# A convolution-attention-expert kernel: two token norms move from GpSimd to ScalarE, the weight products of the opening move behind the first projections, and 35 instead of 41 outward products are plain

## The chip, the cores and the metric

The kernel runs on one core of a Trainium2 chip. The metric is device time in microseconds, median of several runs. The engines are TensorE (PE in the profile; PEld is its weight load), VectorE (DVE), ScalarE (ACT), GpSimd (POOL) and SyncE (SP, which issues most DMAs). Each runs its own instruction stream; they wait for each other by semaphores.

## The reference

Input x is 4 images of 128 channels by 1024 positions, float32. Per image:

1. Group norm over 32 groups of 4 channels, projections q, k, v, full attention of 1024 by 1024 (softmax over 1024 keys), output projection, residual: `x + Wp(softmax(q k / sqrt(C)) v)`.
2. The 1024 positions become tokens `t`. `t = t + attn(ln(t))` with a linear attention of 4 heads: softmax of the keys over the tokens, a context of 32 by 32 per head, output weights and bias b_out.
3. `t = t + moe(ln(t))`: with w = ln(t), 8 experts, router softmax, the best two kept and normed to 1, `out = w + sum_e share_e * (gelu(w W1_e + b1_e) W2_e + b2_e)`. `ln` is `(v - mean) / sqrt(var + 1e-5)` over the 128 channels of a token.

So the first token norm gives `u` (from t1), the second one gives `w_n` (from t2), and `t2 + w_n` is the residual that the experts' sum is added to.

## The kernel before

Tokens of an image are 8 tiles of 128 tokens (TILES = 8, QUAD = 4 of them in a half of 512). Most products are made in two parts, a float32r high part and a low part (value minus high part): `product3` (L1344) issues three matmuls of 512 columns, hi*hi, hi*lo, lo*hi. A "plain" product is one float32 matmul, which the trace records twice.

**Setup and batch 0.** TensorE makes the group means and variances of image 0, then products without use (`keep_busy`, L1373, two records each), then the transpose of Wv, the product `wpv` = Wv Wp and the column `bias_o` (L1385 to L1391), `keep_busy` again, and waits for the first low half of h. Batch b then projects q and k (L1535 to L1544), and for each of 8 score tiles TensorE makes scores (L1409), VectorE the row maximum (L972), ScalarE the exponential (L665), TensorE the transposes (L1418), ScalarE the high copy (L671), VectorE the low part (L977); `attend` (L1423) multiplies with v. Batch 0 also carries the group norm statistics of images 1 to 3: `group_stats`, `channel_means`, `group_deviation`, `group_variance`, `group_affine` on VectorE (L866 to L899), two small products on TensorE, `group_rstd` on GpSimd (L513).

**Pipelining.** Batch b carries the linear attention of image b-1 and the norm, logits and routing of image b-2. GpSimd computes the group-normed input of the next batch (`norm_x`, L527), `add_bias`, and the two token norms: `layer_norm` (L543) makes three small columns (L549 to L553) and then 8 tile instructions (L557); `normed_residual` (L565) adds w_n to t2; `add_bout` (L572) adds the bias. Order within each engine is that of the code.

**Expert stage.** 64 steps, 16 per image (half h, expert e). Step s: TensorE's `hidden` (L1615) into one of two score banks, which needs the gelu of step s-2; then `outward` (L1625) of step s-5 (LAG = 5); ScalarE's `gelu` (L797); VectorE's `weigh` (L1230, gelu times the share of the expert). If the step is not in WHOLE, ScalarE's `high` (L805) and VectorE's `lower` (L1249) make the two parts and `outward` is a product3; if it is in WHOLE, `outward` is plain (L1636). What remains of images 2 and 3 (linear attention, second norm, logits, routing) is put between the steps by the tables TAIL_AT and END_AT: a name and the step behind which each engine does its part of it. POOL_AT orders GpSimd's part the same way, though it only sets an order, since GpSimd takes no part in the steps. Names: PV attend, o output of the linear attention, st the second norm's statistics, OT and OTst the attention output and the first norm's statistics, w0/w1 and u0/u1 the transposes of w_n and u, lg logits, lT logits transposed, rA, rB, rC routing, kT keys, exp both exponentials (another table than gelu's), p transposes of the keys' exponential, g and c the context and the combine weights, z the residual's transposes. Combine weights are stored to DRAM and loaded back as shares, broadcast over the partitions (SyncE, L414).

## Time and profile before

| what | us |
|---|---|
| median of 3 runs (345.7 to 347.02) | 346.47 |
| the profiled execution's own time | 347.13 |
| span of its trace | 345.4 |
| TensorE busy | 310.6 |
| VectorE busy | 248.0 |
| ScalarE busy | 186.4 |
| GpSimd busy | 101.7 |

The span is from the first to the last instruction; the execution's own time has some 1.7 us around it. Times in rows are microseconds from the span's start. A matmul's end is modelled, so TensorE's busy time is not its work at full speed: records of 0.39 us that start every 0.23 us are one after another. The clock column is the granted TensorE clock as a share of 2.4 GHz. Idle time stands in brackets, with what ended it.

### The profile page before, as it was taken

The page shows a single profiled execution, that of the slowest core. Times are in us where ns is not written, and L with a number is a line of the kernel's source. Part 1 is how long each engine was busy: PE and PEld are TensorE (multiplying, and loading weights), DVE is VectorE, ACT ScalarE, POOL GpSimd, SP SyncE. Part 2 cuts the span into 40 slices and gives each one's busy share as a digit, 9 for nine tenths or more (in the row PEclk, how much of TensorE's full clock was granted, in tenths as well). Part 3 has the DMA queues.
Part 4 walks back from the last instruction along what each step waited for, and adds up shares of the span by engine and source line. Part 5 has one row for each costly group of instructions (what it writes and reads, how often), then busy time and mean ns, then how long its engine had stood idle before and what let it go on. Part 6 is the DMA issues. An engine that isn't in the chain of part 4 may idle for free.

```text
span 345.4 us, 5132 instructions
## 1 busy us (share of the span) xinstructions
PE 310.6 (90%) x1573; PEld 240.4 (70%) x1573; DVE 248.0 (72%) x574; ACT 186.4 (54%) x323; POOL 101.7 (29%) x154
## 2 busy tenths in 40 slices
PE   3969998979989889888988998999999997799996
PEld 2858776867878777676877786866557655466784
DVE  4977557497478598978688877597396576846995
ACT  1427546357462568346176658335466334745883
POOL 3806700029400944700446200059420055000000
PEclk9998998998999999999999999999999999989999
DMA  6701000010000020100000108295410691278111
GB/s 176 260 1 62 0 1 2 0 61 3 0 2 1 0 63 9 53 13 0 0 0 0 61 14 261 83 415 198 161 62 0 215 373 47 61 284 325 58 39 61
DMA packets 12756, 29.57 MB, mean 86 GB/s; under 512 B 2192, under 2 KB 5952, under 8 KB 10816
## 3 DMA queue, kind: packets, MB, share of 16 engines
q1 hardware_dynamic: 11872, 29.00, 23.6%
q10 hardware_dynamic: 864, 0.33, 0.4%
q8 instruction: 10, 0.16, 0.2%
q14 instruction: 10, 0.08, 0.1%
HBM read 24.73 MB, written 4.59 MB: 85 GB/s over the span
## 4 chain that ended last, share of the span: by engine, by line
PE 56%; DVE 21%; ACT 8%; issue 7%; POOL 6%; DMA 1%; DVEq 0%; POOLq 0%; ACTq 0%
PE ring L1347 7%; PE ring L1348 6%; PE ring L1349 6%; PE ring L1362 6%; PE scores L1347 5%; PE scores L1349 5%; PE scores L1348 5%; PE ring L1636 5%; DVE row_max L974 5%; DVE pT_lo L980 3%; ACT prob L668 2%; POOL w_n L557 2%; PE ring L1496 2%; DVE lst L1010 2%; ACT pT_hi L674 2%
## 5 line engine op out<-in xcount | busy, mean ns | idle before, releaser
L802 ACT ACTIVATE gel<-scores,b_c 128x512 f32<-128x512 f32 x64 | 43.6, 688 | 44.1 <-PE scores L1349 40.2
L980 DVE TENSOR_TENSOR pT_lo<-ring,pT_hi 128x512 fp32r<-128x512 f32 x64 | 41.2, 683 | 21.0 <-ACT pT_hi L674 20.7
L668 ACT ACTIVATE prob<-scores,row_max 128x1024 f32<-128x1024 f32 x32 | 35.8, 1118 | 25.7 <-DVE row_max L974 25.7
L974 DVE TENSOR_REDUCE row_max<-scores 128x1 f32<-128x1024 f32 x32 | 38.8, 1214 | 11.6 <-PE scores L1349 11.6
L549 POOL TENSOR_SCALAR rstd<-lmv 128x8 f32<-128x8 f32 x8 | 2.2, 270 | 148.5 <-DVE lmv L1016 148.4
L1362 PE MATMUL ring<-ident,prob 128*128 128x128 f32 x256 | 37.1, 287 | 8.0 <-DVE pT_lo L980 2.6
L1362 PEld LDWEIGHTS ring<-ident,prob 128*128 128x128 f32 x256 | 30.5, 147 | 14.1 <-issue 4.1
L674 ACT ACTIVATE pT_hi<-ring 128x512 fp32r<-128x512 f32 x64 | 35.1, 596 | 7.7 <-PE ring L1362 7.6
L1347 PE MATMUL scores<-wT_hi,w_hi 128*128 128x512 f32 x64 | 36.5, 570 | 0.0
L1347 PE MATMUL scores<-k_both,q_hi 128*128 128x512 f32 x64 | 28.2, 441 | 1.0 <-DVE k_both L964 1.0
L1347 PE MATMUL ring<-pT_hi,v_hi 128*128 128x512 f32 x64 | 26.8, 418 | 0.3 <-issue 0.2
L1348 PE MATMUL scores<-k_both,q_hi 128*128 128x512 f32 x64 | 25.9, 404 | 0.0
L1349 PE MATMUL scores<-k_both,q_lo 128*128 128x512 f32 x64 | 25.8, 403 | 0.0
L1349 PE MATMUL scores<-wT_hi,w_lo 128*128 128x512 f32 x64 | 25.5, 398 | 0.0
L1348 PE MATMUL scores<-wT_lo,w_hi 128*128 128x512 f32 x64 | 25.4, 397 | 0.0
L1349 PE MATMUL ring<-pT_hi,v_lo 128*128 128x512 f32 x64 | 25.0, 390 | 0.0
L1348 PE MATMUL ring<-pT_lo,v_hi 128*128 128x512 f32 x64 | 24.9, 390 | 0.0
L678 ACT ACTIVATE o_s<-ring 128x512 f32<-128x512 f32 x8 | 4.8, 598 | 31.6 <-PE ring L1349 31.6
L1347 PEld LDWEIGHTS scores<-wT_hi,w_hi 128*128 128x128 f32 x64 | 12.2, 191 | 7.6 <-issue 5.3
L557 POOL TENSOR_SCALAR w_n<-t,rstd 128x128 f32<-128x128 f32 x32 | 16.8, 539 | 0.9 <-POOL rstd L553 0.9
L1348 PEld LDWEIGHTS scores<-wT_lo,w_hi 128*128 128x128 f32 x64 | 12.3, 192 | 6.4 <-issue 5.5
L1636 PE MATMUL ring<-h_f,w_s 128*128 128x512 f32 x32 | 16.3, 591 | 0.0
(278 smaller groups left out, 707.7 us busy)
## 6 DMA issues: line engine op xcount, KB each, us to landing
pT_hi<-scratch_s SPq DMA_DIRECT2D x8, 1024.0 KB, 5.7
prob<-scratch_s SPq DMA_DIRECT2D x4, 1024.0 KB, 7.1
k_both<-scratch_s SPq DMA_DIRECT2D x3, 1024.0 KB, 6.3
z_in<-scratch_z SPq DMA_DIRECT2D x8, 256.0 KB, 3.0
out_dram<-out_s SPq DMA_DIRECT2D x8, 256.0 KB, 2.2
xb<-in_x_dram SPq DMA_DIRECT2D x3, 512.0 KB, 3.3
scratch_z<-out_s SPq DMA_DIRECT2D x2, 512.0 KB, 2.8
k_both<-scratch_s SPq DMA_DIRECT2D x4, 256.0 KB, 4.5
```

What stands on the lines that cost most here:

```text
L557: last = pool.tensor_scalar(dst[:, j, :], src[:, j, :], neg[:, j:j + 1], std[:, j:j + 1], ALU.add, ALU.mult)
L668: act.activation(prob[:, i % 2, :], scores[:, 2 * (i % 2):2 * (i % 2) + 2, :].rearrange("p a t -> p (a t)"), ACT.Exp, bias=row_max[:, i:i ...
L674: act.activation(tile_group(pT_hi, n, i), as_tiles(ps(place, unit)), ACT.Copy).then_inc(p_hi_made, 1)
L802: act.activation(half(gel, s % 2), scores[:, s % 2, :], ACT.Gelu, bias=b1_c[:, s % E:s % E + 1]).then_inc(e_gelu, 1)
L974: dve.tensor_reduce(row_max[:, i:i + 1], scores[:, 2 * (i % 2):2 * (i % 2) + 2, :].rearrange("p a t -> p (a t)"), AX.X, ALU.max, negate=Tr ...
L980: dve.tensor_tensor(tile_group(pT_lo, n, i), as_tiles(ps(place, unit)), tile_group(pT_hi, n, i).bitcast(FP32), ALU.subtract).then_inc(drai ...
L1010: last = dve.bn_stats(lst[:, j, :], src[:, j, :])
L1347: pe.matmul(dst, lh, rh, start=start, stop=False)
L1348: pe.matmul(dst, lh, rl, start=False, stop=False)
L1349: return pe.matmul(dst, ll, rh, start=False, stop=stop)
L1362: last = pe.transpose(dst[0:t.shape[-1], j * step:j * step + rows], t, ident[0:rows, 0:rows])
L1636: last = pe.matmul(dst, tile(w2_s, e), hs_ring[step % RING], start=False, stop=e == E - 1)
```

## The change

The columns of the two token norms stay on GpSimd in the expert stage (`norm_small`); the tiles are made on ScalarE, as an activation Identity with the column 1/std as scale and -mean/std as bias, in halves of four tiles (`norm_half`, at aw0, aw1, au0, au1). The residual `t2 + w_n` is made on ScalarE too, from t2 with the scale 1/std + 1 and the same bias (`normed_residual`, az), without reading w_n. In batches 1 to 3 GpSimd does the norms as before. In the opening, the three weight products move behind the first projections, ten `keep_busy` products stand in one row, and the group norm of images 1 to 3 moves to later tiles of batch 0. GpSimd's `group_rstd` for these moves behind both expert splits. ScalarE's exponential 1 of batch 0 stands ahead of its v copies. The tables of the expert stage are new, and WHOLE has 35 steps instead of 41. The diff, cut:

```diff
-SETUP_UNITS = ["gn_mean", "gn_var", "wvT", "wpv", "bias_o"]
+SETUP_UNITS = ["gn_mean", "gn_var"]
...
-TAIL_AT = dict(m3=0, PV=1, o=2, st=5, OT=6, OTst=6, w0=12, w1=13, lg=14, u0=15, u1=19, lT=18, rA=19, kT=20, exp=21, rB=21, ks=21, z=19, p=22, rC=23, g=24, c=25)
-END_AT = dict(ctx=25, m2=27, m3=28, o=29, st=29, w0=34, w1=35, lg=36, lT=36, rA=36, exp=37, rB=36, rC=38, z=39, c=39)
+TAIL_AT = dict(m3=0, PV=0, o=2, st=2, OT=5, OTst=5, w0=11, w1=11, lg=13, u0=13, u1=13, lT=15, rA=16, kT=19, exp=19, rB=19, ks=22, z=16, p=20, rC=19, g=22, c=23,
+               aw0=5, aw1=7, au0=9, au1=9, az=8)
+END_AT = dict(ctx=25, m2=27, m3=28, o=29, st=29, w0=34, w1=34, lg=36, lT=38, rA=38, exp=38, rB=38, rC=39, z=41, c=41,
+              aw0=32, aw1=33, az=35)
...
-POOL_AT = dict(n2=4, n1=9, nr=8, ab=18, n2e=30, nre=38)
-
-
-WHOLE = frozenset((2, 3, 4, 5, 6, 7, 8, 9, 10, 11, 12, 13, 14, 15, 16, 17, 18, 19, 20, 21, 22, 23, 24, 25, 26,
-                   27, 28, 29, 30, 31, 32, 33, 34, 37, 38, 39, 40, 42, 43, 44, 45))
+POOL_AT = dict(n2=0, n1=1, ab=2, n2e=3)
+
+
+WHOLE = frozenset((2, 3, 4, 5, 6, 7, 8, 11, 12, 14, 15, 16, 17, 22, 23, 24, 26, 27, 28, 29, 30, 32, 33, 34,
+                   35, 36, 37, 38, 39, 40, 42, 43, 44, 45, 47))
...
+            def norm_small(n, lb):
+
+                eps, std, neg = (rstd[n][:, i, :] for i in range(3))
+                pool.wait_ge(ln_stats[n], lb + 1)
+                pool.tensor_scalar(eps, lmv[n][:, :, 1], 1.0, LN_EPS, ALU.mult, ALU.add
+                                   ).then_inc(ln_small[n], 1)
+                pool.tensor_scalar(neg, lmv[n][:, :, 0], -1.0, 0.0, ALU.mult, ALU.add)
+                pool.wait_ge(ln_small[n], lb * 2 + 1)
+                pool.tensor_tensor(std, eps, minus_half[:, :], ALU.pow).then_inc(ln_small[n], 1)
+                pool.wait_ge(ln_small[n], lb * 2 + 2)
+                after(pool.tensor_tensor(eps, neg, std, ALU.mult))
+                if n == 1:
+                    after(pool.tensor_scalar(neg, std, 1.0, 1.0, ALU.mult, ALU.add))
+                pool.sem_inc(ln_ready[n], 1)
...
-            wait_drained(pool, SETUP, "bias_o")
+            wait_drained(pool, FIRST, "bias_o")
...
-                if name == "w1":
-                    group_rstd(FIRST, 1, B - 1)
...
+            group_rstd(FIRST, 1, B - 1)
...
-                (POOL_AT["n2"], lambda: second_norm(B - 2)),
-                (POOL_AT["n1"], lambda: first_norm(B - 1)),
-                (POOL_AT["nr"], lambda: normed_residual(B - 2)),
+                (POOL_AT["n2"], lambda: norm_small(1, B - 2)),
+                (POOL_AT["n1"], lambda: norm_small(0, B - 1)),
                 (POOL_AT["ab"], lambda: add_bout(B - 1, TAIL)),
-                (POOL_AT["n2e"], lambda: second_norm(B - 1)),
-                (POOL_AT["nre"], lambda: normed_residual(B - 1)),
+                (POOL_AT["n2e"], lambda: norm_small(1, B - 1)),
...
+            def norm_half(n, times, src, dst, g, made):
+
+                act.wait_ge(ln_ready[n], times)
+                shift, std = rstd[n][:, 0, :], rstd[n][:, 1, :]
+                for j in range(g * QUAD, (g + 1) * QUAD):
+                    last = act.activation(dst[:, j, :], src[:, j, :], ACT.Identity, bias=shift[:, j:j + 1],
+                                          scale=std[:, j:j + 1])
+                last.then_inc(made, 1)
+
+            def normed_residual(lc):
+                shift, std_and_one = rstd[1][:, 0, :], rstd[1][:, 2, :]
+                act.wait_ge(w_made, lc * HALVES + HALVES)
+                for j in range(TILES):
+                    last = act.activation(t2[:, j, :], t2[:, j, :], ACT.Identity, bias=shift[:, j:j + 1],
+                                          scale=std_and_one[:, j:j + 1])
+                last.then_inc(z_made, 1)
...
+                *((TAIL_AT["aw" + str(n)], lambda n=n: norm_half(1, 1, t2, w_n, n, w_made)) for n in range(2)),
+                *((TAIL_AT["au" + str(n)], lambda n=n: norm_half(0, 1, t1, u, n, u_made)) for n in range(2)),
+                (TAIL_AT["az"], lambda: normed_residual(lc)),
+                *((END_AT["aw" + str(n)], lambda n=n: norm_half(1, 2, t2, w_n, n, w_made)) for n in range(2)),
+                (END_AT["az"], lambda: normed_residual(la)),
...
-            wait_filled(dve, SETUP, "wvT")
-            dve.tensor_copy(wvT[:, :], tile(ps(SETUP, "wvT"), 0)).then_inc(drained[SETUP.bank("wvT")], 1)
             low_first()
-            wait_filled(dve, SETUP, "wpv")
-            dve.tensor_copy(wpv[:, :], tile(ps(SETUP, "wpv"), 0)).then_inc(drained[SETUP.bank("wpv")], 1)
-            wait_filled(dve, SETUP, "bias_o")
-            dve.tensor_tensor(bias_o, ps(SETUP, "bias_o")[:, 0:1], bp_c, ALU.add
-                              ).then_inc(drained[SETUP.bank("bias_o")], 1)
+            group_stats(1)
...
-                    for n in range(1, B - 1):
-                        group_stats(n)
...
-                    group_stats(B - 1)
-                    channel_means(1, B - 1)
...
-                    project_v(place, b)
-                    group_deviation(place, 1, B - 1)
...
+                    merge_weights()
                 row_maximum(b, 1)
+                if la is None:
+                    group_stats(2)
-                    setup_rest()
+                    project_v(place, b)
                 turn_probs(place, b, 0)
                 row_maximum(b, 2)
+                    setup_rest()
                 turn_probs(place, b, 1)
+                if la is None:
+                    group_stats(3)
+                    channel_means(1, B - 1)
                 row_maximum(b, 3)
                 turn_probs(place, b, 2)
                 row_maximum(b, 4)
+                if la is None:
+                    group_deviation(place, 1, B - 1)
                 turn_probs(place, b, 3)
                 row_maximum(b, 5)
+                if la is None:
+                    group_variance(place, 1, B - 1)
+                if la is None:
+                    group_affine(2, 1, B - 1)
...
-            keep_busy(6)
-            pe.wait_ge(ld_w["wv"], 16)
-            turn(SETUP, "wvT", [wv_s[:, :]])
-            keep_busy(2)
-            wait_drained(pe, SETUP, "wvT")
-            pe.wait_ge(ld_w["wp"], 16)
-            small(SETUP, "wpv", C, wvT[:, :], wp_s[:, :])
-            pe.wait_ge(ld_w["cols"], 64)
-            small(SETUP, "bias_o", 1, wp_s[:, :], bv_c)
-            keep_busy(6)
+            keep_busy(10)
...
+                if la is None:
+                    pe.wait_ge(ld_w["wv"], 16)
+                    turn(place, "wvT", [wv_s[:, :]])
...
+                    wait_drained(pe, place, "wvT")
+                    pe.wait_ge(ld_w["wp"], 16)
+                    small(place, "wpv", C, wvT[:, :], wp_s[:, :])
+                    pe.wait_ge(ld_w["cols"], 64)
+                    small(place, "bias_o", 1, wp_s[:, :], bv_c)
+                    score(b, 1)
+                    wait_drained(pe, place, "wpv")
                     project_v(place)
-                    group_means(place, 2, 1, B - 1)
-                    score(b, 1)
                 else:
                     attend(place, 1, QUAD, TILES)
                     score(b, 1)
                     turn_o(place, 1)
                     project_v(place)
+                turn_probs(place, b, 0)
+                score(b, 2)
                 if la is None:
                     pe.wait_ge(ld_w["qkv"], 16)
                     turn(place, "l1qT", [wqkv_s[:, 0:C]])
                     pe.wait_ge(ld_w["rows8"], 32)
                     turn(place, "routerT", [rows8[:, 0, :]], rows=E)
                     turn(place, "b1T", [rows8[:, 1, :]], rows=E)
-                    group_variances(place, 2, 1, B - 1)
```

## Rows read from the trace of the kernel before

**Rows 1.** The page's first section: busy us and share of the span by engine.

```profile
PE 310.6 (90%) x1573; PEld 240.4 (70%) x1573; DVE 248.0 (72%) x574; ACT 186.4 (54%) x323; POOL 101.7 (29%) x154
```

**Rows 2.** Windows by stage: busy us of TensorE (two), then of ScalarE; instructions, clock, DMA.

```profile
232.00:262.00 30.00, 28.98 (x119) 1.00 0.35 136
...
283.00:306.00 23.00, 18.03 (x74) 0.93 0.29 101
...
226.00:240.00 14.00, 6.61 (x10) 1.00 0.77 312
```

**Rows 3.** Windows of TensorE around its stops; columns as in rows 2.

```profile
22.40:25.90 3.50, 1.06 (x7) 1.00 0.01 2
...
25.90:29.30 3.40, 3.40 (x13) 0.51 0.02 5
...
283.50:285.50 2.00, 0.64 (x2) 1.00 0.99 359
...
298.60:301.50 2.90, 0.58 (x6) 1.00 0.41 120
...
301.50:305.20 3.70, 3.63 (x12) 0.63 0.67 236
```

**Rows 4.** Timeline of TensorE late in the expert stage: start us, us, instruction, idle before.

```profile
285.57 0.66 PE L1362 MATMUL scores<-ident,w_n 128*128 128x128 f32 x4 [1.43 <-POOL w_n L557]
...
301.57 0.33 PE L1362 MATMUL ring<-ident,comb 128*128 128x128 f32 x1 [2.39 <-DVE comb L1133]
```

**Rows 5.** Timeline of the opening; columns as in rows 4.

```profile
7.52 2.91 PE L1377 MATMUL scores<-ident,group_mean 128*128 128x128 f32 x12
...
13.48 0.48 PE L1347 MATMUL ring<-h_hi,wq_hi 128*128 128x512 f32 x1
...
19.50 1.17 DVE L974 TENSOR_REDUCE row_max<-scores 128x1 f32<-128x1024 f32 x1
```

**Rows 6.** Timeline of VectorE, the last pT_lo before attend.

```profile
37.09 1.29 DVE L980 TENSOR_TENSOR pT_lo<-ring,pT_hi 128x512 fp32r<-128x512 f32 x2 [0.39 <-ACT pT_hi L674]
```

**Rows 7.** Timeline of GpSimd.

```profile
38.48 2.54 POOL L536 TENSOR_TENSOR h_lo<-h_f,h_hi 128x512 fp32r<-128x512 f32 x2 [0.18 <-POOL h_hi L531]
...
228.43 1.64 POOL L553 TENSOR_TENSOR rstd<-rstd,minus_half 128x8 f32<-128x8 f32 x1
...
287.32 2.37 POOL L567 TENSOR_TENSOR t<-t,w_n 128x1024 f32<-128x1024 f32 x1
```

**Rows 8.** Timeline of TensorE at the start of batch 1.

```profile
50.97 0.47 PE L1347 MATMUL ring<-h_hi,wq_hi 128*128 128x512 f32 x1
```

**Rows 9.** Timeline of TensorE: hidden products of following steps, outward plain, then split.

```profile
226.87 0.80 PE L1347 MATMUL scores<-wT_hi,w_hi 128*128 128x512 f32 x1
...
228.43 0.79 PE L1347 MATMUL scores<-wT_hi,w_hi 128*128 128x512 f32 x1
...
324.58 0.40 PE L1347 MATMUL scores<-wT_hi,w_hi 128*128 128x512 f32 x1
...
325.95 0.39 PE L1347 MATMUL scores<-wT_hi,w_hi 128*128 128x512 f32 x1
```

**Rows 10.** Timeline of TensorE, first attend product of the expert stage.

```profile
212.87 0.47 PE L1347 MATMUL ring<-pT_hi,v_hi 128*128 128x512 f32 x1
```

**Rows 11.** ScalarE's groups by form: shapes, count, busy us, mean ns, idle before.

```profile
L802 ACT ACTIVATE gel<-scores,b_c 128x512 f32<-128x512 f32 x64 | 43.6, 688 | 44.1 <-PE scores L1349 40.2 <-DVE hs L1247 1.7 <-DVE h_f L1247 1.5
...
L668 ACT ACTIVATE prob<-scores,row_max 128x1024 f32<-128x1024 f32 x32 | 35.8, 1118 | 25.7 <-DVE row_max L974 25.7
...
L652 ACT ACTIVATE h_hi<-xb,gadd,gmul 128x512 fp32r<-128x512 f32 x2 | 1.5, 808 | 4.7 <-DVE gadd L898 4.7
...
L719 ACT ACTIVATE rt<-rt 128x64 f32<-128x64 f32 x4 | 1.1, 273 | 0.0
```

**Rows 12.** Timeline of VectorE late in the expert stage.

```profile
279.45 0.64 DVE L1016 BATCH_NORM_AGGREGATE lmv<-lst 128x2 f32<-128x6 f32 x8 [0.16 <-DVE lst L1010]
...
287.68 2.55 DVE L1247 TENSOR_TENSOR hw<-gel,k_both 128x512 f32<-128x512 f32 x1
```

More of the change, by code:

```diff
@@ L56, in attention_units @@
     return (
-        T[6] * L + ["ctx"] * R + ["q0"] + T[7] * L + ["m2"] * R + ["k0", "k1"] + ["m3"] * R + ["q1"]
+        T[6] * L + ["ctx"] * R + ["q0"] + T[7] * L + ["m2"] * R + ["k0", "k1"] + ["wvT"] * (not L) + ["m3"] * R
+        + ["q1"] + ["wpv", "bias_o"] * (not L)
         + ["PV1"] * L + ROUTING["o"] * R + ["OT1"] * L + ATTENTION["v"]
-        + ["gn_mean", "l1qT", "routerT", "b1T", "gn_var"] * (not L) + T[0]
+        + T[0] + ["l1qT", "routerT", "b1T"] * (not L)
         + T[1] + ATTENTION["xT"]
         + ROUTING["w"] * R + T[2]
-        + ROUTING["lg"] * R + T[3] + LINEAR["u"] * L
+        + ["gn_mean"] * (not L) + ROUTING["lg"] * R + T[3] + ["gn_var"] * (not L) + LINEAR["u"] * L
         + ["lT"] * R + ROUTING["z"] * R + LINEAR["kT"] * L + ["PV0"] + T[4]
@@ L286, in conv_attention_moe @@
         ln_small = [sem(f"ln_small{n}") for n in range(2)]
+        ln_ready = [sem(f"ln_ready{n}") for n in range(2)]
         u_made, w_made, z_made, t1b_made = sem("u_made"), sem("w_made"), sem("z_made"), sem("t1b_made")
@@ L745, in batch @@
                 softmax(b, 0)
-                if la is not None:
-                    softmax(b, 1)
+                softmax(b, 1)
                 project_v(place)
-                if la is None:
-                    softmax(b, 1)
                 turn_probs(place, 0)
@@ L933, in _, with merge_weights @@
             dve.tensor_scalar(bqs_c, bq_c, SCALE, None, ALU.mult).then_inc(setup_made, 1)
-            wait_filled(dve, SETUP, "wvT")
-            dve.tensor_copy(wvT[:, :], tile(ps(SETUP, "wvT"), 0)).then_inc(drained[SETUP.bank("wvT")], 1)
             low_first()
-            wait_filled(dve, SETUP, "wpv")
-            dve.tensor_copy(wpv[:, :], tile(ps(SETUP, "wpv"), 0)).then_inc(drained[SETUP.bank("wpv")], 1)
-            wait_filled(dve, SETUP, "bias_o")
-            dve.tensor_tensor(bias_o, ps(SETUP, "bias_o")[:, 0:1], bp_c, ALU.add
-                              ).then_inc(drained[SETUP.bank("bias_o")], 1)
+            group_stats(1)
+            def merge_weights():
+                wait_filled(dve, FIRST, "wpv")
+                dve.tensor_copy(wpv[:, :], tile(ps(FIRST, "wpv"), 0)).then_inc(drained[FIRST.bank("wpv")], 1)
+                wait_filled(dve, FIRST, "bias_o")
+                dve.tensor_tensor(bias_o, ps(FIRST, "bias_o")[:, 0:1], bp_c, ALU.add
+                                  ).then_inc(drained[FIRST.bank("bias_o")], 1)
             def setup_rest():
@@ L1145, in batch @@
                     turn_probs(place, la, 6)
-                else:
-                    for n in range(1, B - 1):
-                        group_stats(n)
                 project(place, b, "q0", q_hi, q_lo, bqs_c)
@@ L1155, in batch @@
                 project(place, b, "k1", k_hi, k_lo, bk_c)
+                if la is None:
+                    take(place, "wvT", wvT[:, :])
                 if lc is not None:
@@ L1158, in batch @@
                 project(place, b, "q1", q_hi, q_lo, bqs_c)
-                if la is None:
-                    group_stats(B - 1)
-                    channel_means(1, B - 1)
                 if la is not None:
@@ L1178, in batch @@
                 else:
-                    setup_rest()
-                    group_variance(place, 1, B - 1)
+                    project_v(place, b)
                 turn_probs(place, b, 0)
@@ L1183, in batch @@
                 if la is None:
-                    group_affine(2, 1, B - 1)
+                    setup_rest()
                 if la is not None:
@@ L1541, in batch @@
                 project(place, b, "k1", wk_hi, wk_lo)
+                if la is None:
+                    pe.wait_ge(ld_w["wv"], 16)
+                    turn(place, "wvT", [wv_s[:, :]])
                 if lc is not None:
@@ L1569, in batch @@
                     turn(place, "b1T", [rows8[:, 1, :]], rows=E)
-                    group_variances(place, 2, 1, B - 1)
-                turn_probs(place, b, 0)
-                score(b, 2)
                 turn_probs(place, b, 1)
@@ L1582, in batch @@
                 score(b, 4)
+                if la is None:
+                    group_means(place, 2, 1, B - 1)
                 if lc is not None:
@@ L1586, in batch @@
                 score(b, 5)
+                if la is None:
+                    group_variances(place, 2, 1, B - 1)
                 if la is not None:
```

## The prediction, made before the changed kernel was run

> **What bounds the kernel now.** I read four views. The page's busy rows first: TensorE is busy 90% of the span, no other engine over 72% [rows 1]. So work off TensorE matters only where TensorE stands still or runs at its half clock. The windows by stage say where, from the expert stage on: between 232 and 262 us it lacks 1.0 us of 30, between 283 and 306 it lacks 5.0 of 23 [rows 2]. The windows of TensorE around its stops show what follows an idle stretch. After 22.4 to 25.9, with 1.06 us of work in 3.50, the granted clock is 0.51 (the 1.2 GHz level) for 3.4 us. After 298.6 to 301.5 (0.58 of 2.90) it is 0.63 over 3.7 us. In 283.5 to 285.5 (0.64 of 2.00) it stays at 1.00, 2.4 GHz [rows 3]. The timeline names what TensorE waited for late in the kernel: 1.43 us for GpSimd's w_n and 2.39 us for the combine weights [rows 4].
>
> The sum is made against the profiled execution: 347.13 us, span 345.4. The median of the runs is 346.47, 0.66 lower; the sum is subtracted from the median.
>
> **A. The opening, projections first.** Six keep-busy products, twelve records, took 2.70 us up to 10.22, 0.213 us per record after the first; the first projection started at 13.48 [rows 5]. Now ten products stand there and no weight product between them: 8 more records, 1.70 us, end at 11.92. The low half of the first input is ready before that (VectorE's wvT copy ahead of it is gone). I charge 0.25 us for first matmuls that are still at the half clock of those records: gain 1.3. VectorE also no longer has one bn_stats pair (1.3 us) and the aggregate (0.35) ahead of the first row maximum, which started at 19.50 [rows 5]; the scores are now there near 17.7: gain 1.75. From there I walk on with the old durations: row maximum 1 at 19.6, both exponentials done by 22.1, v_lo by 23.8, the first probabilities split by 25.1, the second by 28.5, then bn_stats of image 3 and the aggregate, row maximum 3 at 30.05, and 2.1 to 3 us a tile as before. The last pT_lo ahead of the attend product then ends near 35.6, where it ended at 37.09 + 1.29 = 38.38 [rows 6]: 2.8 us. That walk has the full clock. TensorE is again short of work, from 23.5 to 26.5 (2.4 of 3.0 us idle, held by VectorE's drains), a stretch like the one that 0.51 followed [rows 3]; if the clock falls, score 3 comes 0.95 us after VectorE wants it. I take half of that: **-2.3 us**, bounds -1.0 (the first projections wholly at the half clock, and score 3 too) and -2.8.
>
> What hides the moved group norm: GpSimd's normalisation of image 1 ended its low half at 41.0 [rows 7]. The affine columns now come after row maximum 5, about 38.8, so h_lo ends near 44.5. TensorE needed it at 50.97 [rows 8], 48.7 after the shift: 4 us of cover. GpSimd's queue stands at bias_o until 19.2 instead of 12.7; its two expert splits behind it then end by 28, and nobody waits for them before the end of batch 0. SyncE's order is the same, and batches 1 to 3 have the same code, so the gain passes through.
>
> **B. Expert stage, steps 0 to 30.** A step is one hidden product and the outward one of five steps before.
> - Outward products. A step with a plain one takes 228.43 - 226.87 = 1.56 us, with a split one 325.95 - 324.58 = 1.37 [rows 9]: 0.19 less on TensorE, one more copy on ScalarE and one more subtraction on VectorE. Nine become split (9, 10, 13, 18 to 21, 25, 31), three plain (35, 36, 47). Seven of the nine fall here: -1.3.
> - attend moves from step 1 to step 0. It waits for the last pT_lo; TensorE started it at 212.87, with a hidden product done inside the wait [rows 10]. Now that product stands behind it: +0.65.
> - The norms. ScalarE gets 24 instructions of 128x128 with two pointer operands at steps 5 to 9 (aw0, aw1, az, au0, au1), a form that the trace does not show. The nearest row is h_hi, 128x512 with both pointers, 808 ns; prob against gel, one pointer each, gives (1118 - 688)/512 = 0.84 ns a column, so 384 columns fewer leave 0.49 us; back-to-back records overlap by 0.09, hence 0.40 [rows 11]. Lower bound 0.26 (the 128x64 exponential without pointers, 273 ns [rows 11]), upper 0.49 without overlap. I take 0.40, as h_hi is nearest in form. The Trainium skill ("ScalarE: Activation LUTs", What ACT_TABLE_LOAD costs) has 186 ns + 0.833 ns a column + 93 ns a pointer, with 93 overlapped; no row shows this form, and an estimate by that page is 0.386, 9.3 us for 24.
>  The statistics come early now (step 3, about 222.7); GpSimd's columns take 2.1 us, of which the power is 1.64 [rows 7], and two small ones more: ready at 225.8. ScalarE waits for them from 224.35. From there it is one chain: 24 tiles, 9.6 us, and five gelus at 0.6, to 238.2, where it had 7.4 us free between 226 and 240 [rows 2]. A hidden product needs the gelu two steps back: step 8 loses 0.4, step 11 1.8, step 12 1.4, so +3.6 (tile at 0.26: +1.0; at 0.49: +5.8).
> - Keys and exponential are both at step 19, with two table loads between two gelus: TensorE waits 0.6 at step 20. Its old idle time up to step 30, 1.0 [rows 2] and 0.9 in short gaps, goes: together -1.3.
>  **+1.6 us** (0.65 + 3.6 - 1.3 - 1.3).
>
> **C. Steps 30 to 63.** Times from the start of step 30, 276.1 in the old run. The last batch's statistics end at 279.45 + 0.64 [rows 12], +4.0; the columns are ready at +7.8. ScalarE stands at aw0 from +5.2, gives half 0 at +9.45, a gelu, half 1 at +11.6. TensorE is done with outward 29 at +7.75, has both turns of w_n at step 34 and waits 1.75 and 1.75. Then the logits, the routing on VectorE, and a wait of 0.4 for the combine weights at step 41. Gone are w_n's stop 1.6 and the comb stop 2.5 (0.1 to 0.2 of it for the modelled ends) [rows 4], the rest of the 5.0 us, 1.3, which is the logits', and the low clock behind the comb stop, 0.37 x 3.7 = 1.4 [rows 3]: -6.8 + 3.9 = **-2.9 us**. Step 47 plain: **+0.2**.
>  The logits' stop was VectorE's: one multiply took 2.55 us where its like takes 0.69, from 287.68, while GpSimd's add ran from 287.32 [rows 7, 12]. That add leaves GpSimd. The skill has a rule for it in "SBUF — State Buffer" (Who interferes with whom): a VectorE instruction with two SBUF inputs and a GpSimd one that reads SBUF exclude each other. By that rule the trace agrees; the add of b_out stays on GpSimd and can still do it once.
>  New: TensorE is idle 3.5 of 3.9 us from +7.75, a stretch of the kind that a low clock followed [rows 3]. Its next 3.4 us would then do half the work; of the 1.7 lost 0.8 is hidden behind gelu 36: **+0.9** (bounds 0 and 1.7).
>  The shares of batch 3 are stored by +31 and land about 4.5 later; step 48 multiplies at +37.6: 2 us of cover. SyncE's queue has the same order.
>
> **Sum.** -2.3 + 1.6 - 2.9 + 0.2 + 0.9 = -2.5. 346.47 - 2.5 = **344.0 us**.
>
> **The rivals.**
> 1. The norms are cheap (a tile at 0.26 to 0.30) and the clock holds. For: 2 us of near idleness at 283.5 without a fall [rows 3]. Against: the two-pointer row. 2.3 comes off steps 8 to 12, 0.9 for the clock, 0.4 for half 1 of w_n: 344.0 - 3.6 = 340.4; with a part of it, 341 to 342.
> 2. The opening gives only 1.0 us, since low clock follows idle time there as before: 345.3. For: 0.51 in the old run [rows 3]. Against: TensorE has more work in those 3 us than it had.
> 3. Slower: the gelus' queue. Place: ScalarE at steps 5 to 12 and 19 to 22, where norms, split copies and table loads stand ahead of the gelu that TensorE needs next. A tile at 0.49 makes the chain 2.2 longer; TensorE is then idle for over half of steps 10 to 12 and falls to 1.2 GHz (+1.6); the copies of steps 18 to 21 behind the table loads add 1.0, the end 0.4. 344.0 + 5.2 = 349.2. It decides from 0.46 us a tile, where the chain alone takes 1.4 more and the low clock follows. Against: 0.09 of overlap is seen on every pair of ScalarE's records.
> 4. It does not do what it says if ScalarE's norms stand behind GpSimd's columns as the old ones did: that wait is in the sum (1.5 and 2.6 us of ScalarE), so it is no case of its own.
>
> **Chances.** Forecast 0.43, own range 342.4 to 345.6; rival 1 0.25 (340.2 to 342.4); rival 2 0.18 (344.7 to 346.5); rival 3 0.14 (347 to 350). Range of 8 in 10: 340.7 to 347.4. About 0.5% (1.7 us) is what can be told from no change. Faster than 344.7: 0.35 + 0.25 + 0.02 = 0.62. Within it: 0.08 + 0.16 + 0.02 = 0.26. Slower than 348.2: 0.12.
>
> **What would show it.** First projection near 11.9, first row maximum near 17.8, the pT_lo before attend done at 35.6 to 36.6. Norm tiles 0.40 us from start to start; TensorE waiting for gelus at steps 8, 11 and 12, 3.6 us together; VectorE multiplies over 1 us once at most. Near the end TensorE idle twice for 1.7 us before w_n's turns, then a granted clock well under 1.00, and the comb wait under 0.6 instead of 2.39. I am wrong if batch 1 starts less than 1 us earlier, if the tiles cost under 0.3 or over 0.46, or if TensorE waits for shares at step 48.

## The result, and the profile after

The changed kernel takes 344.96 us (median of 17 runs, 342.58 to 346.41); the kernel before, beside it, 346.86 (17 runs). The ratio is 0.994, interval 0.9915 to 0.9965: 0.35 to 0.85% faster, and 1.0 us above the forecast of 344.0. The gain between the medians is 1.9 us, where 2.5 was forecast. The profiled execution took 344.23 us, its span is 342.5.

The page of the changed kernel: busy time by engine, then the granted clock of TensorE by slices of 8.6 us. ScalarE took on 17 us [rows 1], GpSimd gave up 16. The clock has one deep dip, in slice 34, and a shallower one in slice 7.

```profile
PE 306.3 (89%) x1571; PEld 238.6 (70%) x1571; DVE 248.3 (72%) x580; ACT 203.6 (59%) x369; POOL 85.4 (25%) x133
...
PEclk9999998999999999999999999999999996999999
```

The opening, timeline of the changed kernel (start us, us, instruction, idle before). They answer to rows 5, 6 and 8: the first projection is 1.86 us earlier, the first row maximum 2.23, the last pT_lo before attend ends at 34.91 instead of 38.38, batch 1 starts 3.41 earlier.

```profile
7.61 4.02 PE L1419 MATMUL scores<-ident,group_mean 128*128 128x128 f32 x20
...
11.62 0.47 PE L1389 MATMUL ring<-h_hi,wq_hi 128*128 128x512 f32 x1
...
17.27 1.22 DVE L1011 TENSOR_REDUCE row_max<-scores 128x1 f32<-128x1024 f32 x1 [0.54 <-PE scores L1391]
...
33.63 1.28 DVE L1017 TENSOR_TENSOR pT_lo<-ring,pT_hi 128x512 fp32r<-128x512 f32 x2
...
47.56 0.47 PE L1389 MATMUL ring<-h_hi,wq_hi 128*128 128x512 f32 x1
```

ScalarE and TensorE in steps 5 to 12. ScalarE waits for GpSimd's columns, then makes 24 tiles with the gelus in between; the hidden products of steps 11 and 12 wait for those gelus.

```profile
222.00 1.65 ACT L716 ACTIVATE w_n<-t,rstd 128x128 f32<-128x128 f32 x4 [1.15 <-POOLq L579]
...
226.81 3.18 ACT L724 ACTIVATE t<-t,rstd 128x128 f32<-128x128 f32 x8
229.89 0.67 ACT L832 ACTIVATE gel<-scores,b_c 128x512 f32<-128x512 f32 x1
230.46 3.18 ACT L716 ACTIVATE u<-t,rstd 128x128 f32<-128x128 f32 x8
...
230.61 0.50 PE L1389 MATMUL scores<-wT_hi,w_hi 128*128 128x512 f32 x1 [1.40 <-ACT gel L832]
...
234.26 0.50 PE L1389 MATMUL scores<-wT_hi,w_hi 128*128 128x512 f32 x1 [0.95 <-ACT gel L832]
```

The last batch's chain, answering to rows 4: GpSimd's columns, ScalarE's halves, TensorE's turns (transposes) of w_n, the turn of the combine weights.

```profile
278.80 2.10 POOL L574 TENSOR_TENSOR rstd<-rstd,minus_half 128x8 f32<-128x8 f32 x1
...
281.55 1.65 ACT L716 ACTIVATE w_n<-t,rstd 128x128 f32<-128x128 f32 x4 [2.87 <-POOLq L579]
...
283.25 0.66 PE L1404 MATMUL scores<-ident,w_n 128*128 128x128 f32 x4 [1.93 <-ACT w_n L716]
...
283.67 1.64 ACT L716 ACTIVATE w_n<-t,rstd 128x128 f32<-128x128 f32 x4
...
285.36 1.12 PE L1404 MATMUL scores<-ident,w_n 128*128 128x128 f32 x4 [1.46 <-ACT w_n L716]
...
302.84 0.33 PE L1404 MATMUL ring<-ident,comb 128*128 128x128 f32 x1 [0.30 <-DVE comb L1170]
```

Windows of TensorE in the changed kernel (stretch, us, busy, granted clock, DMA). The first answers to the first of rows 3, and no low clock comes right after it; the next low stretch is in the second line. The last three are around w_n's turns. The clock fell at the end of the first turn (up to 283.90 it reads 1.00), before the second wait, and it stayed low for 6.8 us, twice the 3.4 of rows 3.

```profile
22.40:25.90 3.50, 1.96 (x11) 1.00 0.01 2
...
51.80:55.30 3.50, 3.50 (x9) 0.51 0.02 5
...
283.20:286.10 2.90, 1.40 (x8) 0.63 0.04 17
286.00:290.50 4.50, 4.50 (x11) 0.50 0.00 0
...
283.90:290.80 6.90, 5.45 (x14) 0.51 0.01 5
```

To see where time goes, I take the start of a hidden product as a mark: step 0, 30, 42 and 63. Every kernel ends 8.3 us after step 63, so these marks hold the whole span.

| profiled execution | step 0 at | steps 0 to 30 | 30 to 42 | 42 to 63 | 0 to 63 |
|---|---|---|---|---|---|
| before | 210.96 | 65.15 | 30.08 | 30.90 | 126.13 |
| after | 207.29 | 66.16 | 29.58 | 31.20 | 126.94 |
| after less before | -3.67 | +1.01 | -0.50 | +0.30 | +0.81 |

The whole gain of 2.9 us in the profile stands ahead of the expert stage, which itself has become 0.8 longer.

### The profile page after: what moved, and what is told of

It reads as the page before. It is cut to its first block, busy times and chain, and to the rows that moved or that the text cites. A ratio compares the mean times of both kernels' runs of the same rounds, so it can differ in the third digit from the quotient of the medians.

```text
span 342.5 us, 5172 instructions
## 1 busy us (share of the span) xinstructions
PE 306.3 (89%) x1571; PEld 238.6 (70%) x1571; DVE 248.3 (72%) x580; ACT 203.6 (59%) x369; POOL 85.4 (25%) x133
## 2 busy tenths in 40 slices
DMA packets 12757, 29.58 MB, mean 86 GB/s; under 512 B 2192, under 2 KB 5952, under 8 KB 10816
## 4 chain that ended last, share of the span: by engine, by line
PE 54%; DVE 24%; ACT 11%; issue 7%; POOL 2%; DMA 1%; DVEq 0%; ACTq 0%; POOLq 0%
PE ring L1389 7%; PE ring L1390 7%; PE ring L1391 7%; DVE row_max L1011 6%; PE scores L1389 6%; PE scores L1391 5%; PE scores L1390 5%; PE ring L1680 5%; PE ring L1404 5%; DVE pT_lo L1017 5%; ACT prob L684 2%; PE ring L1529 2%; DVE lst L1047 2%; ACT gel L832 2%; ACT w_n L716 2%
## 5 line engine op out<-in xcount | busy, mean ns | idle before, releaser
L684 ACT ACTIVATE prob<-scores,row_max 128x1024 f32<-128x1024 f32 x32 | 35.7, 1117 | 23.4 <-DVE row_max L1011 23.2
L1404 PE MATMUL ring<-ident,prob 128*128 128x128 f32 x256 | 35.1, 276 | 9.1 <-DVE pT_lo L1017 3.6
L1404 PEld LDWEIGHTS ring<-ident,prob 128*128 128x128 f32 x256 | 28.6, 140 | 14.8 <-ACT prob L684 4.6
L1389 PE MATMUL scores<-k_both,q_hi 128*128 128x512 f32 x64 | 27.2, 426 | 0.4 <-DVE k_both L1001 0.4
L1390 PE MATMUL scores<-k_both,q_hi 128*128 128x512 f32 x64 | 25.1, 391 | 0.0
L595 POOL TENSOR_TENSOR t<-t,bout_row 128x1024 f32<-128x1024 f32 x4 | 9.5, 2370 | 25.3 <-PE scores L1404 16.5
```

Source lines behind the costliest of these rows:

```text
L595: pool.tensor_tensor(t2[:, :, :], t1[:, :, :], bout_b, ALU.add).then_inc(t1b_made, 1)
L684: act.activation(prob[:, i % 2, :], scores[:, 2 * (i % 2):2 * (i % 2) + 2, :].rearrange("p a t -> p (a t)"), ACT.Exp, bias=row_max[:, i:i ...
L1389: pe.matmul(dst, lh, rh, start=start, stop=False)
L1390: pe.matmul(dst, lh, rl, start=False, stop=False)
L1404: last = pe.transpose(dst[0:t.shape[-1], j * step:j * step + rows], t, ident[0:rows, 0:rows])
```

## The experiments

All kernels were timed in five rounds beside the kernel before; ratios are to it.

### The two halves of the change

The changed opening with the old expert stage (tables, set of plain products, norms on GpSimd), and the other way round:

```diff
# opening only, against after
-TAIL_AT = dict(m3=0, PV=0, o=2, st=2, OT=5, ...)   and END_AT, POOL_AT, WHOLE
+TAIL_AT = dict(m3=0, PV=1, o=2, st=5, OT=6, ...)   all as before
-(POOL_AT["n2"], lambda: norm_small(1, B - 2)), ...  and ScalarE's norm_half, normed_residual
+(POOL_AT["n2"], lambda: second_norm(B - 2)), ...
# experts only: the same lines the other way, against before
```

> The new opening (projections first, group norm later) with the expert stage of before. My theory: the whole gain is the opening's, and the expert stage as changed gives nothing. Then the first hidden product starts at 207.3 us, 3.6 earlier than before, the combine stop at the end with its low clock is as before, and the kernel gains 2.5 to 3.7 us (ratio 0.989 to 0.993), as much as or more than the full change. Rival: opening and expert stage share the gain; then this one gains 1 us or less (ratio above 0.997).

> The opening of before with the new expert stage (norms on ScalarE, new tables, 35 plain products). My theory: TensorE's stops only change their cause, so the time from the first hidden product to the end is 135 us against 134.4 before, and the kernel is within 1 us of before (ratio 0.998 to 1.004). Rival: the expert stage carries 1 to 2 us of the gain, ratio 0.994 to 0.997.

Measured: the opening alone 343.57 us (6 runs, ratio 0.9905, 0.9873 to 0.9938), the expert stage alone 347.11 (12 runs, 1.0002, 0.9978 to 1.0026). From step 0 to 63 they took 126.08 and 126.04 us, the kernel before 126.13. So the opening is the whole gain, and the new expert stage, norms and tables together, is worth nothing. Step 0 of the opening alone started at 209.11, not at the 207.3 expected. Its 3.5 us are more than the whole change's 1.9, but at a granted clock of 0.990 the two kernels take 343.0 to 343.6 and 342.6 to 343.2 us: the difference is how often the clock fell.

In the profile of the opening-only kernel attend started at 36.82, in that of after at 35.06. The windows of TensorE in the former, around its idle stretch behind score 2, show the difference: the clock falls here, as it did before [rows 3], and did not in after's profile.

```profile
23.70:27.70 4.00, 2.31 (x12) 0.86 0.01 2
27.70:30.00 2.30, 2.30 (x12) 0.51 0.00 0
```

The expert stage alone shows the same of its own code. Its profile has the waits of after before w_n's turns (1.95 and 1.46 us, after 1.93 and 1.46), but the low clock behind them lasted 3.4 us instead of 6.8, and steps 30 to 42 took 28.70 us instead of 29.58. Window of TensorE in this kernel:

```profile
290.80:294.30 3.50, 3.50 (x9) 0.51 0.00 0
```

### The change with the 41 plain products of before

```diff
-WHOLE = frozenset((2, 3, 4, 5, 6, 7, 8, 11, 12, 14, ... 45, 47))
+WHOLE = frozenset((2, 3, ... 34, 37, 38, 39, 40, 42, 43, 44, 45))   # the 41 of before
```

> The full change, but with the 41 plain steps of before. My theory: six more plain steps cost TensorE 6 x 0.19 = 1.1 us and free ScalarE of the copies behind the norms, which gives about 0.5 back: 0.3 to 1.1 us slower than the full change. Rival (ScalarE's queue is the limit from step 8 to 36, so that split copies are what costs): 0.5 us or more faster than the full change.

Measured: 345.19 us (11 runs, 0.9943, 0.9921 to 0.9964), against 0.994 for after. Steps 0 to 30 took 67.39 us, 1.23 more than after's 66.16: the price of plain products is there as the rows had it (1.3). Steps 30 to 42 took 27.70 instead of 29.58, with waits for w_n of 1.33 and 1.46 us and no low clock behind them, as its windows of TensorE show:

```profile
284.00:289.00 5.00, 2.22 (x12) 1.00 0.16 64
289.00:293.00 4.00, 4.00 (x15) 1.00 0.00 0
```

So this profile does not price the plain products of the second half. The medians put all six at 0.2 us, less than the 0.3 to 1.1 expected, but they stand at different clocks: 9 of the 11 runs have a mean granted clock of 0.990 or more, of after's 17 only 3. At 0.990 this kernel took 344.6 to 345.7 us and after 342.6 to 343.2; at 0.984 and 0.985 it took 344.9 and 345.5, after 344.1 to 345.0. So the six products do cost something, from under 1 to over 2 us by these few runs, and the clock hid it. Why the clock fell less often here is not shown.

### w_n's last turns later

```diff
-END_AT = dict(..., w0=34, w1=34, lg=36, lT=38, ...)
+END_AT = dict(..., w0=35, w1=36, lg=37, lT=38, ...)
```

> The full change with the last batch's turns of w_n and its logits one and two steps later (w0 35, w1 36, lg 37), so that TensorE has hidden products to do while ScalarE makes the two halves. My theory: TensorE no longer stands 2.1 and 2.0 us at step 34 with a clock at 1.2 GHz behind it; the two idle stretches shrink to under 1.5 us together, the low clock at 286 to 290 goes, and step 42 starts 1.5 to 2.5 us earlier. Rival: the combine weights bind step 41, since logits and routing come later; TensorE then waits 2 us or more for comb and the time is the full change's within 0.5 us.

Measured: 342.83 us (6 runs, 0.9886, 0.9853 to 0.9919). Steps 30 to 42 took 27.90 us, 1.68 less than in after, as the theory had it. But the wait did not go, it moved from w_n to a gelu that stands behind ScalarE's halves, and a low clock is still behind it, for 3.4 us instead of 6.8. That is about what was won. The runs say the same: at a granted clock of 0.990 this kernel took 342.6 and 343.1 us, after 342.6 to 343.2. Timeline and window of TensorE in this kernel:

```profile
285.08 0.50 PE L1389 MATMUL scores<-wT_hi,w_hi 128*128 128x512 f32 x1 [2.51 <-ACT gel L832]
```

```profile
285.60:289.10 3.50, 3.50 (x10) 0.51 0.00 0
```

### ScalarE's blocks cut up, then the last chain later too

```diff
-               aw0=5, aw1=7, au0=9, au1=9, az=8)
+               aw0=5, aw1=7, au0=9, au1=10, az0=12, az1=14)
-END_AT = dict(..., w0=34, w1=34, lg=36, lT=38, ..., rC=39, z=41, c=41, aw0=32, aw1=33, az=35)
+END_AT = dict(..., w0=35, w1=36, lg=37, lT=38, ..., rC=39, z=41, c=41, aw0=32, aw1=33, az0=36, az1=38)   # spread
+END_AT = dict(..., w0=37, w1=38, lg=39, lT=41, ..., rC=42, z=44, c=44, aw0=34, aw1=35, az0=39, az1=41)   # spread, late
```

> The kernel after, with the turns of w_n at steps 35 and 36 and the logits at 37 as in the run before this one that had them there, and ScalarE's blocks of 3.2 us cut up: u's halves at steps 9 and 10 instead of both at 9, and the residual (8 tiles) in two halves at steps 12 and 14 instead of 8 (36 and 38 instead of 35 for the last batch). Theory (the stalls of steps 11 and 12, 1.55 and 1.10 us, are gelus that stand behind those blocks in ScalarE's queue): most of the 2.65 us goes, hidden product 12 starts 1.5 to 2.5 us sooner after product 8, and the time is 342.83 less 1.5 to 2.5 = 340.3 to 341.3. Rival (the stalls are the wait for GpSimd's columns, or the half tiles only arrive later for the turns of u): the waits move to the turns of w_n and u at steps 11 to 13 and to z at 16, and the time stays at 342.5 to 343.5.

> As the kernel that cuts ScalarE's blocks up, and the whole chain of the last batch two steps later: its norm halves at steps 34 and 35 instead of 32 and 33, the turns of w_n at 37 and 38, logits 39, router 41, its weights at 44. Theory (in the last batch ScalarE waits 2.87 us for GpSimd's columns while gelus stand behind it; two steps are 3 us): the stalls of steps 30 and 31, 2.65 and 0.82 us in the kernel with the later turns, go, no low clock follows, and the time is 2.5 to 4 us below the kernel with the blocks cut up alone: 337 to 339. Rival (the chain is as long as it is: the wait reappears at the logits or at the comb turn, and the transfer of the last weights is late for the outward bias product of step 53): 1 us or less is won, 340 to 342, with a new wait of over 1.5 us at step 44 or 53.

Measured: cut up, 343.32 us (12 runs, 0.9918, 0.989 to 0.9946), no better than the 342.83 without. By the rows, the waits of steps 11 and 12 fell from 2.35 to 0.37 us, but others of 0.81 (step 13) and 0.57 (the turns of z) came; steps 0 to 21 took 47.51 us instead of 47.94. The time is the rival's: the tiles cost ScalarE the same wherever they stand, and the waits moved with them.

With the last chain later, 346.34 us (12 runs, 0.9995, 0.997 to 1.002), far above what either side expected. The profile is of its fastest run (343.62, clock 0.995). Steps 30 to 42 took 21.92 us, 7.7 less than in after, as the theory had it; and steps 42 to 63 took 38.65, 7.5 more. About 1.2 us of both is only the turns of z and of the weights, which now stand behind mark 42; the rest is a wait. In this kernel VectorE's multiply of step 48 waits for its shares, and TensorE for the combine weights that are queued behind 3 MB of them:

```profile
312.11 1.29 DVE L1291 TENSOR_TENSOR hs<-gel,k_both 128x512 f32<-128x512 f32 x2 [3.25 <-DMA k_both<-scratch_s]
...
320.12 0.47 PE L1678 MATMUL ring<-cb_in,b_parts 128*128 128x512 f32 x1 [3.52 <-DMA cb_in<-scratch_c]
```

### The price of the low clock

Five products that nothing reads, into the bank of w_n's first turn:

```diff
             def turn_w(place, lb, n):
+                if place is END:
+                    spare = open_unit(place, f"w{n}")
+                    for _ in range(5 if n == 0 else 0):
+                        pe.matmul(spare[:, 0:C], group_mean[:, :], ident[:, :], start=True, stop=True)
                 pe.wait_ge(w_made, lb * HALVES + n + 1)
```

> The kernel after, with five products of the group matrix and the identity, which nothing reads, written to the bank of w_n's first turn of the last batch before TensorE waits for w_n there (a wait of 1.97 us, in which TensorE stands still, with the granted clock near half behind it, 286 to 290.5). Theory (the clock falls because TensorE stands still there, and its price is 1.0 to 1.5 us): the clock stays up at 286 to 290 and the time is 343.5 to 344. Rival (the stall of 2.08 us just ahead is enough to bring the clock down, or the products run past the end of the wait and cost what they save): 344.5 to 345.5, and the clock low as before.

Measured: 343.03 us (6 runs, 0.9903, 0.9871 to 0.9936), 0.5 below the theory's range; the interval overlaps with that of after, so the profile has to speak. The five products are the ten records; the turns are not earlier, and the clock behind them stays at 2.4 GHz. Timeline and windows of this kernel:

```profile
283.05 1.28 PE L1536 MATMUL scores<-ident,group_mean 128*128 128x128 f32 x10
...
285.17 0.66 PE L1404 MATMUL scores<-ident,w_n 128*128 128x128 f32 x4 [0.83 <-ACT w_n L716]
```

```profile
283.00:287.70 4.70, 2.36 (x19) 1.00 0.19 70
287.70:291.00 3.30, 3.30 (x16) 1.00 0.00 0
```

From hidden product 34 to 35 it took 6.63 us (after 6.94), from 35 to 37 4.39 (after 6.58). So the low clock cost after's profile 2.2 us behind the second turn, and 0.3 more up to it. In the runs the gain is the clock too: all six had a mean of 0.988 to 0.993, 14 of after's 17 had 0.979 to 0.985, and at 0.990 both kernels take 343 us. That the five products are what held it is likely and not shown: in the kernel with 41 plain products it held without them, over waits of 1.33 and 1.46 us.

### The norms back on GpSimd

```diff
-                *((TAIL_AT["aw" + str(n)], lambda n=n: norm_half(1, 1, t2, w_n, n, w_made)) for n in range(2)),
-                ...  au, az, END's aw and az
-                (POOL_AT["n2"], lambda: norm_small(1, B - 2)),
+                (POOL_AT["n2"], lambda: second_norm(B - 2)),
+                ...  first_norm, normed_residual, and the last batch's
```

> The kernel after with the norms of the expert stage back on GpSimd, whole, and its other parts (opening, tables of steps, set of plain products) as they are. Theory (ScalarE's halves bring w_n and u some 3 us sooner than GpSimd, and the tables have been set to that): the turns of w_n at step 11 and of u at 13, and those of step 34, wait 2 to 4 us more than with ScalarE's halves, and the time is 348 to 352. Rival (what ScalarE's halves win in the turns they lose in gelus behind them, so that the place of the norms is worth nothing even with these tables): 344 to 346.

Measured: 342.71 us (6 runs, 0.9885, 0.9848 to 0.9921). My theory fell: the time is 5.3 us below the lower end of what it expected, and 1.3 below the rival's. With after's own tables the norms on GpSimd are 2.2 us better by the medians (the two intervals just touch) and about 1.5 at a like clock (0.984: 342.6 against 344.1 to 344.3; 0.990: 340.8 and 341.8 against 342.6 to 343.2). From step 0 to 63 it is 124.48 us instead of 126.94: 1.43 of it up to step 30, 1.07 from 30 to 42. The 1.07 is not the engine's: the low clock lasts 3.4 us here, and the expert stage alone, on ScalarE with 3.4 us of low clock too, took 28.70 against 28.51 here. Timeline of this kernel at the end:

```profile
281.50 3.98 POOL L561 TENSOR_SCALAR w_n<-t,rstd 128x128 f32<-128x128 f32 x8 [0.22 <-POOL rstd L557]
...
283.80 0.66 PE L1401 MATMUL scores<-ident,w_n 128*128 128x128 f32 x4 [2.12 <-POOL w_n L561]
...
285.53 0.80 PE L1401 MATMUL scores<-ident,w_n 128*128 128x128 f32 x4 [1.07 <-POOL w_n L561]
285.56 2.37 POOL L586 TENSOR_TENSOR t<-t,w_n 128x1024 f32<-128x1024 f32 x1
```

GpSimd makes eight tiles in 3.98 us, from 281.50; ScalarE made them from 281.55, a gelu between the halves, and was done at 285.31. The second turn started at 285.53 here and at 285.36 there. A tile on ScalarE is 0.1 us cheaper than one on GpSimd, and the gelu eats that. But in the last batch nothing that TensorE needs stands behind them on GpSimd, which pays once the turns stand later.

### The norms on GpSimd, w_n's last turns later

```diff
-END_AT = dict(..., w0=34, w1=34, lg=36, lT=38, rA=38, ..., rC=39, z=41, c=41)
+END_AT = dict(..., w0=35, w1=36, lg=37, lT=38, rA=38, ..., rC=39, z=41, c=41)   # first
+END_AT = dict(..., w0=36, w1=36, lg=37, lT=39, rA=39, ..., rC=40, z=42, c=42)   # second
+END_AT = dict(..., w0=36, w1=37, lg=38, lT=40, rA=40, ..., rC=41, z=43, c=43)   # third
```

> The kernel after with its expert stage's norms back on GpSimd (342.71 us in the call before) and w_n's two turns of the last batch at steps 35 and 36 and its logits at 37, instead of both at 34 and 36. Theory (w_n is late at step 34 with either engine, and two steps of products cover most of the wait): the turns' waits (2.27 and 1.30 us) shrink to under 1.5 us together, the gate of the low clock goes, and the time is 341.0 to 342.2. Rival (the last batch's chain of logits, router, stores and share loads ends within 1 us of step 48 anyway, so that what is won before is waited for there): 342.3 to 343.2.

> As the kernel with GpSimd norms, with both turns of the last batch's w_n at step 36, logits 37, router 39, its weights at 42 (one step later than after). Theory: hidden product 42 starts some 3 us sooner than with the turns at 34, and the time is 340.5 to 342. Rival (shares of step 48 land some 11 us after the router's weights are made, at 312 to 313): step 48's multiplies wait for them, the wait appears at steps 49 to 52, and the time is 342.3 to 343.5.

> As the kernel with GpSimd norms, turns of the last batch's w_n at steps 36 and 37, logits 38, router 40, its weights at 43 (two steps later). Theory: no wait for w_n is left, hidden product 42 starts 4 to 6 us sooner than with the turns at 34, and the time is 340 to 341.5. Rival (the share loads are the bound from here, as in the ScalarE kernel with its chain two steps later, where VectorE waited 3.25 us for them and TensorE 3.65 us at step 52): the time is 342.5 to 345 with a wait of over 2 us at steps 49 to 53.

Measured: 338.96 us (6 runs, 0.9763, 0.9726 to 0.98); 344.94 (9 runs, 0.9922, 0.9893 to 0.9951); 340.51 (6 runs, 0.9831, 0.9791 to 0.9871).

In the table, "34/34, 41" are the steps of w_n's two last turns and of the combine weights.

| norms on | last turns, weights | 0 to 30 | 30 to 42 | 42 to 63 | us |
|---|---|---|---|---|---|
| ScalarE | 34/34, 41 (after) | 66.16 | 29.58 | 31.20 | 344.96 |
| ScalarE | 35/36, 41 | 66.15 | 27.90 | 31.22 | 342.83 |
| GpSimd | 34/34, 41 | 64.73 | 28.51 | 31.24 | 342.71 |
| GpSimd | 35/36, 41 | 64.73 | 25.09 | 31.22 | 338.96 |
| GpSimd | 36/36, 42 | 64.72 | 22.98 | 38.41 | 344.94 |
| GpSimd | 36/37, 43 | 64.72 | 22.61 | 36.05 | 340.51 |

The fourth row is the fastest kernel of this study, 2.4% below before (2.0 to 2.7), with an interval clear of before's and after's; that of the sixth row overlaps it by a hair. Against the second row only the engine of the norms and of the residual differs: 3.9 us, of which the profiles show 1.42 up to step 30 and 2.81 from 30 to 42. Some 3 us of it stay at a like clock (0.988 to 0.990: 339.4 to 340.0 us against 342.3 to 343.1); the rest is the clock, which fell behind the gelu's wait of 2.51 us there and not behind 0.99 here. The time is 2 us below what the theory expected (341.0 to 342.2): it named both the wait and the low clock and priced them at 0.5 to 1.7 us together, and they gave 3.75. Timeline of this kernel: one wait of 0.99 us is left where after had 1.93 and 1.46, and the clock column of 283 to 306 reads 1.00 (before 0.93 [rows 2]).

```profile
283.46 0.66 PE L1401 MATMUL scores<-ident,w_n 128*128 128x128 f32 x4 [0.99 <-POOL w_n L561]
```

```profile
283.00:306.00 23.00, 21.84 (x91) 1.00 0.27 98
```

The fifth row's time is 1.4 us above even the rival's range. It takes 7.2 us more from 42 to 63, 1.2 of it for the turns that now stand behind mark 42 and 1.4 for a low clock behind the wait (from hidden product 53 to 55 it took 8.53 us, the ScalarE kernel with its chain later, whose clock held, 7.14). Timeline and window of that kernel: the shares of step 48 are late, and so are the combine weights, as in the ScalarE kernel with its chain later.

```profile
312.04 1.29 DVE L1286 TENSOR_TENSOR hs<-gel,k_both 128x512 f32<-128x512 f32 x2 [3.02 <-DMA k_both<-scratch_s]
...
319.93 0.77 PE L1673 MATMUL ring<-cb_in,b_parts 128*128 128x512 f32 x1 [3.35 <-DMA cb_in<-scratch_c]
```

```profile
319.80:323.20 3.40, 3.27 (x8) 0.50 0.85 315
```

Its stores went out at 302.40, 2.8 us later than in the fourth row's kernel (299.59), and its loads 4.7 us behind them instead of 2.4. Why that second interval doubled stays open. In the sixth row's kernel it is 2.7 us and VectorE waits 2.10 us at step 48. There hidden product 42 starts 5.9 us sooner than with the turns at 34, as the theory had it, and the waits of the rival came too (2.10 and, for the combine weights, 2.84 us); the time is the theory's, since less was lost than won.

## Why the prediction was right, and where it was not

The time (344.96) and the sign are within the forecast's own range. The terms, against the profile:

| step | predicted | measured |
|---|---|---|
| A, the opening | -2.3 (-1.0 to -2.8) | -3.67 |
| B, steps 0 to 30 | +1.6 | +1.01 |
| C with its low clock, steps 30 to 42 | -2.0 | -0.50 |
| step 47 plain, steps 42 to 63 | +0.2 | +0.30 |
| sum | -2.5 | -2.86 |

So the sum is close to this profile because two errors of 1.4 and 1.5 us went against each other, and both are for the most part the clock of this one execution. The runs gained 1.9 us, 0.6 less than forecast. That the number came so near is in part luck. The split holds better: the forecast has the opening at -2.3 and the expert stage at -0.2 (1.6 - 2.9 + 0.2 + 0.9), the two halves alone measured -3.5 and nothing.

**A** was right in its mechanism and short in size. The first projection came at 11.62 (said: near 11.9), the row maximum at 17.27 (near 17.8), the last pT_lo ended at 34.91 (the walk with the full clock: 35.6). I had charged the low clock behind the idle stretch at half. It comes or does not. Eleven kernels here have the new opening, with the same instructions in it. In the profiles of six of them attend starts at 35.0 to 35.7, in the other five at 36.6 to 37.2, where before had 38.48. So A is about -3.2 or about -1.7. In before's profile that low clock is in, in after's it is not, and so -3.67 flatters the change: the opening alone, with the low clock in, reaches step 0 1.85 us before the old one. Rival 2 is half true: it is not another course of the change but another execution of it.

**B** was right in its mechanism, and both of its parts were smaller than said. ScalarE's tiles were 0.39 us from start to start (0.40 said; 482 ns each, 0.09 of it overlapped), the chain was 24 of them and five gelus, and TensorE waited for gelus at steps 11 and 12, 1.40 and 0.95 us by the rows, where the walk had 1.8 and 1.4; at step 8, where it had 0.4, there was no wait. So the norms cost 2.35 us instead of 3.6, and what was to come off (0.65 - 1.3 - 1.3) was 1.3 instead of 2.0. An estimate by the formula of the Trainium skill ("ScalarE: Activation LUTs", What ACT_TABLE_LOAD costs) is 0.386 a tile: the trace agrees. Rival 3 with its dear tiles is excluded.

**C** failed in its size. The waits for w_n's halves were there, 1.93 and 1.46 us by the rows against 1.75 and 1.75. The comb wait fell from 2.39 [rows 4] to 0.30, as said. What was off is the term "of the 1.7 lost 0.8 is hidden behind gelu 36: +0.9": the prediction took 3.4 us of low clock behind both waits. The clock fell behind the first one and stood low for 6.8 us, nothing hid it, and it cost 2.2 to 2.5. Even with 3.4 us of it, in the profile of the expert stage alone, C was -1.4 (28.70 against 30.08) and not -2.0.

**What the prediction did not ask.** It priced ScalarE's tiles well and never set them against GpSimd's. It took the wait for GpSimd's w_n as a cost of GpSimd's tiles. It was the cost of where the turns stood: with the norms left on GpSimd and only the tables and the plain products new, the expert stage takes 124.48 us, and with the move to ScalarE 126.04 (the expert stage alone, 3.4 us of low clock at its end as there) or 126.94 (after): 1.6 to 2.5 us of the gain are given back.

The other argument for the move was the add that slows VectorE's multiply [rows 7, 12]. It is real and cheap. The fastest kernel of this study has it, on its timeline of GpSimd and VectorE:

```profile
285.21 2.38 POOL L586 TENSOR_TENSOR t<-t,w_n 128x1024 f32<-128x1024 f32 x1
...
285.57 2.57 DVE L1286 TENSOR_TENSOR hs<-gel,prob 128x512 f32<-128x512 f32 x1
```

A multiply of 0.69 us takes 2.57, and the logits' second half waits 0.36 us for it. By "SBUF — State Buffer" of the Trainium skill (Who interferes with whom) this is to be expected of a VectorE instruction with two SBUF inputs beside a GpSimd instruction that reads SBUF, and the trace agrees; in the kernel with GpSimd norms and the turns at 34 the multiply stood at 288.37, behind the add's end, and took 0.69.

**Cover for the shares.** The prediction gave 2 us of cover for the shares of step 48, with 4.5 us for their way. In after k_both's load was issued at 306.89 and landed 6.1 us later, near 313.0; the multiply started at 314.11. So 1.1 us was left, and every version that won more than that before step 48 without making the combine weights sooner lost it there.

## What to carry to other kernels

Work moved off a slow engine should be priced by what stands behind it on the new one, not by its own duration: here equal tiles cost 2 to 4 us more on the engine whose queue TensorE waits for (1.5 to 3 at a like clock). When a value comes late, first move its consumer: two table entries (turns at steps 35 and 36 instead of 34) were worth as much as the whole change (2.1 us against 1.9, by way of the low clock behind the wait), and nearly twice that once the norms were off ScalarE. And follow the chain to its last transfer before pulling the steps ahead, since what is won ahead of a load that does not get sooner is waited for at the load.

## What the hardware did that I had not expected

The time of one kernel on one core spreads with how often TensorE's clock falls. The 17 runs of after: 342.58 to 343.24 us at a mean granted clock of 0.990, 344.11 to 344.96 at 0.984 to 0.985, 345.36 to 346.41 at 0.979 to 0.980. A fall of 3.4 us at 1.2 GHz, as in rows 3, is 1.7 us lost and 0.005 of the mean over 342 us, and the groups are 1.5 and 1.7 us apart, as if each had one such fall more; that is read from the numbers, since only profiled executions show the stretches. The same idle stretch in the opening was followed by the low clock in five profiles of eleven. The same code and the same two waits before w_n's last turns were followed by 6.8 us of it in after's profile and by 3.4 in that of the expert stage alone. So a single profile prices neither a fall nor its absence, and two kernels are best compared at a like mean clock: the gains of the later turns on ScalarE and of the five products vanish there, that of the norms on GpSimd does not, and the price of the plain products comes out.
